# A mixture-of-experts stage in which a tile's middle transpose and down product come one step later

## The reference, cut to what matters

```python
topk_w, topk_idx = jax.lax.top_k(scores, K)            # K = 2 of 8 experts per token
gp = _leaky(jnp.einsum('th,ehm->etm', x, w_gate))      # M = 128 middle columns
up = jnp.einsum('th,ehm->etm', x, w_up)
y_all = jnp.einsum('etm,emh->eth', gp * up, w_down)
y = (y_sel * topk_w[..., None]).sum(1)                 # plus the shared expert p
```

## Time and profile before

| what | value |
|---|---|
| median of 3 runs | 725.29 us (725.26 to 729.11) |
| the profiled execution | 730.2 us, its span 728.4 us |
| the stage, first `choice_in` to last down product | 460 to 597 us of the span |
| PE busy in the span | 610.7 us (84%) |

### The profile page before, as it was taken

The page is one execution under the profiler, slowest core; times in us unless marked ns, Lnnn a source line. Parts: engine busy times, 40 slices in busy tenths (PEclk is TensorE's granted clock), DMA queues, the critical chain, the costliest instruction groups (busy, mean ns, idle before and its releaser), DMA issues.

```text
span 728.4 us, 12983 instructions
## 1 busy us (share of the span) xinstructions
PE 610.7 (84%) x3606; PEld 478.5 (66%) x3607; DVE 333.3 (46%) x973; ACT 252.0 (35%) x660; POOL 241.0 (33%) x396
## 2 busy tenths in 40 slices
PE   0588888876239999999899988899999989897886
PEld 0467766755216666666789877677787768686665
DVE  3435555444932222364241692244454434575644
ACT  0224333344002222222244422355555534443332
POOL 5201111100011111210371533554454517777830
PEclk9969999999559999999999987999999999899988
DMA  7910000003990111132345700244454432454532
GB/s 161 444 66 1 0 0 0 0 1 115 404 312 23 29 29 43 43 87 72 87 89 168 238 0 23 75 142 141 134 153 135 142 96 83 141 188 152 173 116 75
DMA packets 52067, 79.80 MB, mean 110 GB/s; under 512 B 10998, under 2 KB 43767, under 8 KB 51512
## 3 DMA queue, kind: packets, MB, share of 16 engines
q1 hardware_dynamic: 43864, 57.00, 22.8%
q0 software_dynamic: 8160, 22.29, 11.9%
HBM read 54.09 MB, written 25.17 MB: 109 GB/s over the span
## 4 chain that ended last, share of the span: by engine, by line
PE 61%; DVE 11%; POOL 10%; issue 8%; ACT 4%; DMA 3%; another core or an unknown queue 1%; DVEq 1%; SPq 1%; ACTq 0%; POOLq 0%
PE psum L1451 9%; PE psum L1218 8%; POOL arena L862 8%; PE psum L1236 7%; PE psum L1465 5%; PE psum L1081 5%; PE psum L1107 4%; PE psum L1367 4%; PE psum L1443 2%; PE psum L1101 2%; PE psum L1096 2%; PE psum L1521 2%; PE psum L1377 2%; POOL iota_i L891 2%; PE psum L1357 2%
## 5 line engine op out<-in xcount | busy, mean ns | idle before, releaser
L862 POOL DMA_INDIRECT arena<-x,row_tok x72 | 68.3, 949 | 80.6 <-PE psum L1443 61.2
L862 POOL DMA_INDIRECT arena<-y_sorted,pos_k_i x64 | 65.0, 1016 | 34.2 <-issue 15.1
L1451 PE MATMUL psum<-big_w,arena 128*128 x288 | 73.9, 379 | 0.0
L862 POOL DMA_INDIRECT arena<-h_late,row_tok x16 | 15.3, 959 | 164.8 <-PE psum L1210 98.4
L1521 PE MATMUL psum<-big_w,arena 128*128 x256 | 67.7, 401 | 0.0
L1367 PE MATMUL psum<-arena,big_w 128*128 128x256 f32 x256 | 65.3, 409 | 0.5 <-ACT arena L1783 0.5
L1218 PE MATMUL psum<-big_w,arena 128*128 x128 | 61.8, 628 | 3.7 <-DVE arena L2345 3.7
L1451 PEld LDWEIGHTS psum<-big_w,arena 128*128 128x128 f32 x288 | 54.5, 190 | 7.3
L1236 PE MATMUL psum<-arena 128*128 x256 | 58.0, 379 | 1.5 <-ACT arena L1705 1.5
L1236 PEld LDWEIGHTS psum<-arena 128*128 128x128 f32 x256 | 48.6, 190 | 14.7 <-issue 8.9
L1367 PEld LDWEIGHTS psum<-arena,big_w 128*128 128x128 f32 x256 | 51.4, 206 | 8.5 <-ACT arena L1783 0.9
(11 more groups left out here) (324 smaller groups left out, 1124.8 us busy)
## 6 DMA issues: line engine op xcount, KB each, us to landing
y_sorted<-arena SPq DMA_DIRECT2D x72, 128.0 KB
tokens<-x SPq DMA_DIRECT2D x4, 1024.0 KB, 26.4
x<-tokens SPq DMA_DIRECT2D x16, 256.0 KB, 3.4
z_kept<-arena SPq DMA_DIRECT2D x16, 256.0 KB
out<-arena SPq DMA_DIRECT2D x16, 256.0 KB
y_late<-arena SPq DMA_DIRECT2D x16, 128.0 KB, 1.7
big_w<-expert_w_t SPq DMA_DIRECT2D x1, 2048.0 KB, 7.4
arena<-x,row_tok POOLq DMA_INDIRECT x72
```

What stands on the lines that cost most here:

```text
L862: pool.indirect_dma_start(dst, None, rows, bass.IndirectOffsetOnAxis(ap=idx, axis=0)).then_inc(done, 16)
L1451: mm = pe.matmul(bank[2 + u][:, 0:2 * M1], c_gt[u][:, k, :], mgu_s[:, k, bass.ds(e, 1), :].rearrange("p a m -> p (a m)"), start=k == 0, st ...
```

## The change

Turn and down of a tile follow one step later: in step i PE issues in(i), turn(i-4), down(i-5), up(i-1). DVE's copy of the turn and ACT's copy of the down product move with them. All rings keep their lengths (three buffers each, one bank each for turn and down). The pipeline now drains in five steps, 72 to 76, and the loop of PE holds one expert's number more per turn (16 in place of 15); the load behind the loop has 5 in place of 4.

```diff
-                down, up = not static or 4 <= i, not static or 1 <= i < TILES2 + 1
+                down, up = not static or 5 <= i, not static or 1 <= i < TILES2 + 1
                 if not static or i < TILES2:
                     choice_in(i, u, turn_no)
-                if not static or 3 <= i < TILES2 + 3:
-                    choice_turn(i - 3, u)
+                if not static or 4 <= i < TILES2 + 4:
+                    choice_turn(i - 4, (u - 4) % RT)
                 if down:
-                    choice_down(i - 4, (u - 4) % RT, e_down)
+                    choice_down(i - 5, (u - 5) % RT, e_down)
                 if up:
                     choice_up(i - 1, (u - 1) % RT, e_up)
...
             with pe.Fori(1, TILES2 // GT) as r:
-                e = numbers(tile_e2[0:1, bass.ds(GT * r - 4, GT + 3)], GT + 3)
+                e = numbers(tile_e2[0:1, bass.ds(GT * r - 5, GT + 4)], GT + 4)
...
             def choice_step(i, u):                       # DVE
-                if not static or 3 <= i < TILES2 + 3:
-                    dve.wait_ge(c_mt, i - 2)
-                    dve.tensor_copy(c_midt[u], bank[1][:, 0:M1]).then_inc(c_mtc, 1)
+                if not static or 4 <= i < TILES2 + 4:
+                    dve.wait_ge(c_mt, i - 3)
+                    dve.tensor_copy(c_midt[(u - 4) % RT], bank[1][:, 0:M1]).then_inc(c_mtc, 1)
...
-                if not static or 4 <= i:                 # ACT
-                    w = (u - 4) % RT
-                    if not static or i - 4 >= RT:
-                        hold(act, c_st[w], 16 * (turn_no - (2 if u == 0 else 1)))
-                    hold(act, c_dn, i - 3)
+                if not static or 5 <= i:
+                    w = (u - 5) % RT
+                    if not static or i - 5 >= RT:
+                        hold(act, c_st[w], 16 * (turn_no - (2 if u < 2 else 1)))
+                    hold(act, c_dn, i - 4)
                     act.copy(c_y[w], bank[5][:, 0:D]).then_inc(c_yc, 1)
```

More of the change, by code:

```diff
@@ L1483, in _ @@
             for i in range(GT):
-                choice_step(i, i % RT, i // RT, e[i - 4] if i >= 4 else None, e[i - 1] if i else None)
+                choice_step(i, i % RT, i // RT, e[i - 5] if i >= 5 else None, e[i - 1] if i else None)
             with pe.Fori(1, TILES2 // GT) as r:
-                e = numbers(tile_e2[0:1, bass.ds(GT * r - 4, GT + 3)], GT + 3)
+                e = numbers(tile_e2[0:1, bass.ds(GT * r - 5, GT + 4)], GT + 4)
                 for u in range(GT):
[L1488 to L1491, removed]
+                    choice_step(GT * r + u, u % RT, (GT // RT) * r + u // RT, e[u], e[u + 4])
+            e = numbers(tile_e2[0:1, TILES2 - 5:TILES2], 5)
+            for i in range(5):
+                choice_step(TILES2 + i, i % RT, TILES2 // RT + i // RT, e[i], e[4])
             def turn_z(b, u):
@@ L1793, in _ @@
                     choice_step(RT * r + u, u, r)
-            for i in range(TILES2, TILES2 + 4):
+            for i in range(TILES2, TILES2 + 5):
                 choice_step(i, i % RT, i // RT)
@@ L2586, in _ @@
                     choice_step(RT * r + u, u)
-            for i in range(TILES2, TILES2 + 3):
+            for i in range(TILES2, TILES2 + 4):
                 choice_step(i, i % RT)
```

## The result

The changed kernel took 749.51 us, the median of four runs (748.76 to 754.3), against 726.44 us for the kernel before (725.26 to 729.11): a ratio of 1.0322, 95% interval 1.028 to 1.0363. It is 23 us slower; 727.2 was forecast, with 731.0 as the upper end. The span of its profiled execution is 746.9 us.

The account below looks back on a forecast made before the run. PE was taken to bound the kernel, its late steps waiting for the copy that frees bank 1. Drain 1.44 plus loads 0.5 gave 1.94 us on 725.29: 727.2 us, range 723.5 to 731.0.

Parts of the forecast that it names:

- The wait for c_md: At PE's turn: relaxed but not the last wait to end, 0 us gained; rival that it binds: 720.3 us, chance 0.07.
- Register instructions: One more per DVE loop turn and one in twelve PE steps: 0 us, at most 0.9 and 0.2 us.
- bank 5: The down product waits for ACT's copy of the down product before it, which keeps its place in ACT's order: 0 us.
- The front: Steps 3 and 4 lose a turn and a down product: nothing gained, at most 0.44 us back.
- The drain: Behind the last up product, four down products instead of three, one round more: cost 1.44 us, range 1.0 to 1.72.
- One number more per load: Five loads in PE's loop, each one number longer at 0.10 us a number: cost 0.5 us, range 0.3 to 0.65.
- The load behind the loop: Register load of 4 numbers, 0.346 us, under an up product; one number more still hidden: 0 us.
- The clock: Rival: one more half-clock stretch of TensorE behind the gathers, 3.4 us, giving 730.6 us, chance 0.14.
- The page: Skill page's figure of about 200 ns a register for PE's loads: term 1.0 us, forecast half a microsecond higher; not used.

Follow-up runs that it names:

- g1: Kernel before, with VectorE's copy that frees bank 1 issued between the leaky value and the multiply: 721.32 us against 726.88, ratio 0.9912.
- e7: Kernel before plus a second load of 8 unused numbers in PE's loop, which is not in the traces: 726.13 us against 728.38.
- e1: Kernel before, only the load in PE's loop starts at 12r-5 and takes 16 numbers, the first unused: 758.16 us against 734.74, ratio 1.0349.
- e2: Changed kernel with aligned loads, 19 numbers from 12r-8 and 8 behind the loop; against the kernel before: 736.5 us against 734.74, ratio 1.004.
- d3: Kernel before, with the 15 numbers of a loop turn in two loads, 2 + 13: 753.37 us against 730.51.
- f1: Kernel before, with PE's expert numbers loaded four at a time from multiples of four, one load every four steps: 718.04 us against 726.88, ratio 0.9892.
- e3: Kernel before, with the table of expert numbers in another buffer, one number (4 bytes) further on: 755.92 us against 734.74, ratio 1.0288.
- d2: Kernel before, with the 15 numbers of a loop turn in two loads, 5 + 10: 741.23 us against 730.51.
- d1: Kernel before, with the 15 numbers of a loop turn in two loads, 9 + 6: 740.51 us against 730.51.
- e4: Changed kernel with the table shifted by one number, so its loop loads start aligned; against the kernel before: 733.02 us against 734.74, ratio 0.9979.
- e5: Kernel before, with the load in PE's loop taking 16 numbers from the same start, the last unused: 725.8 us against 728.38, ratio 0.9953.
- e8: Kernel before, with the load starting at 12r-6, a multiple of 8 bytes, and taking 17 numbers: 752.8 us against 728.38.

## Why the prediction was wrong

- *The wait for c_md does not bind.* Right. The turn stays 0.12 us behind the copy, the ten steps stay at 17.4 us, and g1 shows that the copy was the cause of the late steps. The reading of why the copy is late was incomplete. The late copy of the earlier trace rows begins 0.38 us after its multiply began (510.19 - 509.81), the copies of the other two steps 0.20 to 0.21 us after the earlier trace rows. It is the first one in DVE's loop of three, and the loop's own register instructions and its branch (L2584) stand between the two. It is the same in the changed kernel (531.20 - 530.81). So a part of the lateness comes from the turn of DVE's loop; g1 takes the copy away from there, and no run took that part alone.
- *Register instructions, bank 5: nothing.* Right, by the same ten steps.
- *The front: nothing.* Right within what one trace tells: step 5 still begins when its rows are there. The other steps got 1.9 us shorter in sum: 0.8 in steps 0 to 10, which last 17.0 to 18.2 us in traces of kernels that have the same order there (18.2 before, 17.0 in e7), and 1.1 in the loop. In e1, with the old order and holes as long, the loop's part is 0.8. So the change itself is not shown to give any of it.
- *The drain, 1.44 us.* Right: 1.5 us more from the last up to the last down product, 1.47 in e2. The clock that fell there cost 0.5 us on top.
- *One number more per load, 0.10 us.* **This is the step that failed.** The prediction took a slope between a load of 11 numbers and one of 15 for the price of any number more, and read only the count off the diff. The diff also moves the start, from 12r-4 to 12r-5. The loads grew by 2.4 us each, 12.2 us at the five heads, not 0.5. The bound of 0.13 us a number was no bound, since both rows it came from start at a multiple of four. Rows that spoke against a common slope were there: 4 numbers in 0.346 us and 11 in 1.339 are 0.14 a number, while 11 and 15 are 0.10.
- *The load behind the loop is hidden.* Wrong for the same reason: 1.292 us stands out by 0.9 from under the up product.
- *The clock.* The prediction let it fall behind the stage alone, as a rival. It fell inside, at each hole, and that was 9.4 us; the sum had nothing for it. The windows of before did show the clock at 1.00 in the stage with holes of 1.3 us, and nothing in them told how long a hole may be.
- *The page.* The Trainium skill, "Runtime: NRT & Kernel Launch", section "Instruction fetch mechanics", has some 200 ns a register even in bulk; the page has these loads as coming from HBM, the DRAM, and the numbers here lie in SBUF. Loads that start off a multiple of 16 bytes come near that figure, with 0.25 to 0.27 us a number (4.18 / 16, 1.292 / 5); the others do not, with 1.106 us for 16. I had dismissed the page's figure for the smaller slope of my rows. An estimate with it for all 16 numbers, 3.2 us a load against the 1.75 measured before, would have been a rival with a cost of 7 us, and the forecast's range would have been wider.

## What to carry to other kernels

When a hand-written pipeline is shifted by one, read what the shift does to addresses, not to counts alone: an expression such as `12 * r - 4` that becomes `12 * r - 5` changes the alignment of everything that it indexes. A step relaxes a wait only if that wait ends last; look which of the two semaphores at an instruction comes last before giving the other one more room, and move what sits ahead of the late one. Where a loop must load registers at its head, load few, aligned, and while the engine has work queued.

## What the runs showed of the hardware

Loads of 32-bit numbers from SBUF into registers (one instruction, shortest to longest in us; "aligned" is a start at a multiple of four numbers, 16 bytes):

| numbers | aligned | else |
|---|---|---|
| 2 | 0.53 to 0.74 (d3) | |
| 4 | 0.33 to 0.71 (f1) | 1.01 (e3) |
| 5 | 0.59 to 0.75 (d2) | 1.29 (after) |
| 6 | | 1.73 to 1.90 (d1) |
| 8 | 0.60 (e2) | |
| 9 | 0.84 to 0.94 (d1) | |
| 10 | | 2.74 to 2.81 (d2) |
| 11 | 1.34 (before) | 2.64 (e3) |
| 13 | | 3.36 to 3.49 (d3) |
| 15 | 1.59 to 1.86 (before), to 2.07 (g1) | 3.82 to 4.00 (e3) |
| 16 | 1.11 to 1.15 (e4), to 1.29 (e5) | 4.02 to 4.28 (after, e1) |
| 17 | | 4.27 to 4.58 (e8) |
| 19 | 2.06 to 2.39 (e2) | |

An estimate from these lengths: 0.09 us, and 0.25 us for each group of four or, where no group of four starts or is full, each single number. 16 aligned numbers are 4 x 0.25 + 0.09 = 1.09, 16 others 16 x 0.25 + 0.09 = 4.09. The shortest of each kind lies within 10% of it, but for 19 numbers (1.84 against 2.06); the longest are up to a third above it, one of four in f1 twice as long, and why was not looked into. A load that starts off the grid never gets onto it, though at most three single numbers would take it there; and a start at 8 bytes is as dear as one at 4. That fewer numbers can take longer (15 against 16 from the same start, e5) follows from it. That the sequencer reads four registers per access is my reading of these lengths and isn't shown otherwise.

PE's clock stayed at full speed behind every hole of up to 3.8 us from step to step, and fell to half at two of five of 4.1 to 4.5 us and at all from 4.8 us on. As PE's idle time inside the hole, that is full speed up to 1.85 us (e2), half at two of five of 2.1 to 2.5 us (d1, one of them at the shortest of the five), and half at all of 2.8 us and more (d2, d3, after). A load that holds up PE's own stream is enough for it: PE's idle time at these holes ended by "issue", not by another engine.
